# Row sums of a fused attention kernel: one more tile pair summed by DMA in each second half, and the output product moved in front of unit 59

## The reference

```python
Q, K, V = (proj(Wq), proj(Wk), proj(Wv))             # 16 heads of 32 channels
att = jnp.einsum('bhqd,bhkd->bhqk', Q, K) * (1.0 / math.sqrt(Dh)) + b[0]
att = att * m + (1.0 - m) * NEG_INF
att = jax.nn.softmax(att, axis=-1)
y = jnp.einsum('bhqk,bhkd->bhqd', att, V)            # then back to B x 512 x T
q = round(y / scale)                                 # int8 per row, scale = absmax / 127
out = x + float16((q @ weight.T) * scale * w_scale + bias)
```

## Time and profile before

| | |
|---|---|
| median of three runs | 2285.32 us |
| the profiled execution | 2288.77 us |
| its span, first to last instruction | 2287.0 us |
| granted TensorE clock | 0.996 of full |
| busy: TensorE / VectorE / ScalarE / GpSimd | 2264.2 / 1610.9 / 1298.3 / 1686.9 us |
| TensorE matmuls and weight loads | 12140 and 12172 |
| DMA moved | 432.24 MB, of it 166.73 MB in GpSimd's queue |

### The profile page before, as it was taken

The page is one execution under the profiler, slowest core; times in us unless marked ns, Lnnn a source line. Parts: engine busy times, 40 slices in busy tenths (PEclk is TensorE's granted clock), DMA queues, the critical chain, the costliest instruction groups (busy, mean ns, idle before and its releaser), DMA issues.

```text
span 2287.0 us, 34843 instructions
## 1 busy us (share of the span) xinstructions
PE 2264.2 (99%) x12140; PEld 1376.8 (60%) x12172; DVE 1610.9 (70%) x2779; ACT 1298.3 (57%) x2471; POOL 1686.9 (74%) x704
## 2 busy tenths in 40 slices
PE   9999999999999999999999999999999999999998
PEld 7888888887555555555555555555555555555553
DVE  3311111117788888888888888888888888888883
ACT  3322222223666666666666666666666666666664
POOL 2322333222689999899998998989998899899896
PEclk9999999999999999999999999999999999999999
DMA  6765455475788888888888888888888888888864
GB/s 238 254 230 194 177 190 212 183 229 141 157 183 181 194 192 192 191 191 187 188 182 188 191 193 190 188 185 194 191 192 189 187 193 186 179 193 196 189 149 102
DMA packets 146405, 432.24 MB, mean 189 GB/s; under 512 B 13192, under 2 KB 49032, under 8 KB 125904
## 3 DMA queue, kind: packets, MB, share of 16 engines
q1 hardware_dynamic: 114000, 237.31, 36.4%
q0 software_dynamic: 22896, 166.73, 36.3%
q10 hardware_dynamic: 9360, 26.22, 3.4%
HBM read 161.51 MB, written 100.93 MB: 115 GB/s over the span
## 4 chain that ended last, share of the span: by engine, by line
PE 96%; DMA 2%; issue 1%; POOL 1%; ACT 0%; DVE 0%; ACTq 0%; POOLq 0%
PE score L793 22%; PE ring L143 20%; PE pv L819 20%; PE ring L340 11%; PE score L340 9%; PE ring L865 5%; PE pv L340 3%; PE ring L832 2%; DMA probs<-probs 1%; PE ring L830 1%; POOL acc L1145 1%; PE ring L855 1%; PE ring L165 0%; ACT probs L927 0%; PE ring L842 0%
## 5 line engine op out<-in xcount | busy, mean ns | idle before, releaser
L150 DVE TENSOR_REDUCE half_max<-ring 128x1 f32<-128x512 f32 x2048 | 1256.7, 678 | 67.6 <-PE ring L143 59.9
L927 ACT ACTIVATE probs<-score 128x512 f32<-128x512 f32 x2039 | 1033.3, 615 | 471.7 <-PE score L793 466.2
L1145 POOL TENSOR_TENSOR acc<-acc,probs 128x2048 f32<-128x2048 f32 x189 | 898.9, 4756 | 62.5 <-DMA probs<-probs 61.8
L793 PE MATMUL score<-q_stack,k_stack 100*128 100x512 f32 x2039 | 847.6, 417 | 4.7 <-ACT probs L927 4.7
L143 PE MATMUL ring<-k_stack,q_stack 98*128 98x512 f32 x2048 | 816.6, 399 | 2.4 <-issue 2.2
L793 PEld LDWEIGHTS score<-q_stack,k_stack 100*128 100x128 f32 x2039 | 384.4, 189 | 331.8 <-issue 185.5
L819 PE MATMUL pv<-probs,v_in 128*32 128x512 f32 x4096 | 495.0, 601 | 0.0
L143 PEld LDWEIGHTS ring<-k_stack,q_stack 98*128 98x128 f32 x2048 | 389.4, 190 | 70.3 <-DVE qT L1052 8.7
L1145 POOL TENSOR_TENSOR acc<-probs 128x2048 f32<-128x2048 f32 x63 | 288.0, 4571 | 53.9 <-DMA probs<-probs 47.8
L558 POOL TENSOR_TENSOR q_stack<-x_raw,k_stack 128x1024 fp32r<-128x1024 f32 x28 | 67.9, 2471 | 293.9 <-ACT k_stack L422 293.9
L819 PEld LDWEIGHTS pv<-probs,v_in 128*32 128x32 f32 x4096 | 107.1, 109 | 233.1 <-ACT probs L927 145.2
(11 more groups left out here) (117 smaller groups left out, 1986.9 us busy)
## 6 DMA issues: line engine op xcount, KB each, us to landing
probs<-probs POOLq DMA_DIRECT2D x159, 1024.0 KB, 8.3
q_stack<-qk_part SPq DMA_DIRECT2D x192, 256.0 KB, 5.7
k_stack<-qk_part SPq DMA_DIRECT2D x96, 512.0 KB
qk_part<-part_hi SPq DMA_DIRECT2D x64, 512.0 KB, 2.7
qk_part<-part_lo SPq DMA_DIRECT2D x64, 512.0 KB, 3.6
v_steps<-v_out SPq DMA_DIRECT2D x64, 256.0 KB, 2.3
v_in<-v_steps SPq DMA_DIRECT2D x32, 512.0 KB, 5.6
v_out<-x ACTq DMA_DIRECT2D x31, 512.0 KB, 3.5
```

The lines of the kernel that those rows point to most:

```text
L150: nc.vector.tensor_reduce(half_max[:, pair // CHUNK, pair % CHUNK, half:half + 1], bank[:, :], AX_X, ALU.max, negate=True).then_inc(neg_ma ...
L793: pe.matmul(score[score_bank(s, t)][:, :], k_stack[par][0:ROWS, h, kt * P:(kt + 1) * P], q_stack[par][0:ROWS, half, h, :], start=True, sto ...
L927: nc.scalar.activation(probs[:, kt, h, :], score[score_bank(s, t)][:, :], ACT.Exp).then_inc(exp_done, 1)
L1145: nc.gpsimd.tensor_tensor(acc[:, half, :, :], first, probs[:, tile, :, :], ALU.add).then_inc(acc_done, 1)
```

## The change

The pair (2,3) is added to the list of transfers. First halves keep the pairs (0,1), (4,5), (6,7) and their additions. Second halves now transfer (0,1), (2,3), (4,5), and GpSimd adds tiles 6, 3, 5, 7 in that order. TensorE's product with tile 7 goes. GpSimd's order changes around the end of a step. The turned integers move from behind unit 55 to behind unit 54, and the output product from behind unit 59 (after weighing and sums) to behind the maximum of unit 58. The last step takes other banks for its last sums.

```diff
-PAIRS_OF_TILES = ((0, 1), (4, 5), (6, 7))
+PAIRS_OF_TILES = ((0, 1), (2, 3), (4, 5), (6, 7))
+PAIRED = ((0, 2, 3), (0, 1, 2))
-ADDED = ((2, 3, 5, 7), (2, 3, 5, 6))
-APART = 7
+ADDED = ((2, 3, 5, 7), (6, 3, 5, 7))
-TURN_1, SUMS_1, TURN_0, TURN_Q, SUMS_0 = 20, 27, 52, 55, 59
-FFN, SKEW = SUMS_0, SUMS_1
+TURN_1, SUMS_1, TURN_0, TURN_Q, FFN, SUMS_0 = 20, 27, 52, 54, 58, 59
+SKEW = SUMS_1
 EXTRAS = {TURN_1: ("turn",), SUMS_1: ("sums",), TURN_0: ("turn",), TURN_Q: ("turn_q",),
-          SUMS_0: ("unused", "sums", "ffn0", "ffn1")}
+          FFN: ("ffn0", "ffn1"), SUMS_0: ("unused", "sums")}
@@ sum_rows
-                if half == 1:
-                    for h in range(GH):
-                        pe.matmul(buf[h * DH:(h + 1) * DH, 0:N], ones[:, :], probs[:, APART, h, :], start=True, stop=False)
@@ TensorE, step
                     if t == GH - 1 and prev:
                         for kt in (QH * TT - 2, QH * TT - 1):
                             weigh(s - 1, 1 - par, kt)
+                    if t == FFN and prev:
+                        ffn(s - 1)
                     if t % BURST == GH - 1 and t > GH:
...
-                    if t == FFN and prev:
-                        ffn(s - 1)
@@ ScalarE, exps
-                    elif kt in READ_BY:
-                        wait(act, pair_done[READ_BY[kt]], 16 * pairs_before(s, half, READ_BY[kt]))
                     else:
-                        wait(act, sum_done, before + 1)
+                        wait(act, pair_done[kt // 2], 16 * pairs_before(s, half, kt // 2))
@@ GpSimd, step
+                if prev:
+                    add(s - 1, 1, 1)
                 if second:
                     add_bias(s - 2, 0)
                     add_residual(s - 2, 0)
...
                 add(s, 0, 3)
                 if ahead:
+                    begin_pair(s, 1, 1)
+                    begin_pair(s, 1, 2)
                     add(s, 1, 0)
-                    begin_pair(s, 1, 1)
-                    add(s, 1, 1)
```

More of the change, by code:

```diff
@@ L657, in pairs_before, with turned_q @@
         def pairs_before(s, half, i):
-            return s + half if PAIRS_OF_TILES[i][1] == APART else QH * s + half
+            return s * sum(i in paired for paired in PAIRED) + half * (i in PAIRED[0])
+        def turned_q(s):
+            return ("turn", TURN_0) if s >= LAST - 1 else ("turn_q", TURN_Q)
         def ring_of(use):
@@ L827, in sum_rows @@
                 pe.wait_ge(acc_done, ADDS * halves_before(s, half) + ADDS)
-                if half == 1:
-                    for h in range(GH):
-                        pe.matmul(buf[h * DH:(h + 1) * DH, 0:N], ones[:, :], probs[:, APART, h, :], start=True, stop=False)
                 for h in range(GH):
-                    mm = pe.matmul(buf[h * DH:(h + 1) * DH, 0:N], ones[:, :], acc[:, half, h, :], start=half == 0, stop=True)
+                    mm = pe.matmul(buf[h * DH:(h + 1) * DH, 0:N], ones[:, :], acc[:, half, h, :], start=True, stop=True)
                 mm.then_inc(sum_done, 1)
@@ L852, in turn_q @@
                     pe.wait_ge(last_q_done, 1)
-                buf16 = take_ring(s + 1, ("turn_q", TURN_Q))[:, :].bitcast(BF16)
+                buf16 = take_ring(s + 1, turned_q(s))[:, :].bitcast(BF16)
                 for tt in range(TT):
@@ L889, in step @@
                     if not ahead and t == UNITS - 13:
-                        last_sums = take_ring(s, ("sums", SUMS_0))
+                        last_sums = take_ring(STEPS, ("sums", SUMS_1))
                         sum_tile(2, last_sums, start=True)
@@ L894, in step @@
                             sum_tile(tile, last_sums)
-                    if t == FFN and prev:
-                        ffn(s - 1)
                     if not ahead and t == UNITS - 1:
-                        pe.wait_ge(prod_done, 2 * LAST - 1)
-                        sum_rows(s, 0, ring_of(("ffn0", FFN)))
+                        sum_rows(s, 0, take_ring(s, ("sums", SUMS_0)))
                         for kt in (QH * TT - 2, QH * TT - 1):
@@ L1051, in take_qT @@
                 wait(dve, ffn_done, 2 * s)
-                nc.vector.tensor_copy(qT[:, :, :].rearrange("p a b -> p (a b)"), ring_of(("turn_q", TURN_Q))[:, :].bitcast(BF16)[:, 0:T]).then_inc(qT_out, 1)
+                nc.vector.tensor_copy(qT[:, :, :].rearrange("p a b -> p (a b)"), ring_of(turned_q(s))[:, :].bitcast(BF16)[:, 0:T]).then_inc(qT_out, 1)
             def scale_product(s, half):
@@ L1086, in step @@
                         take_qT(s - 1)
-                    if t == SUMS_0 and ahead:
-                        recip(s, 0, ring_of(("sums", t)))
                     if t == FFN and prev:
@@ L1091, in step @@
                             scale_product(s - 1, half)
+                    if t == SUMS_0 and ahead:
+                        recip(s, 0, ring_of(("sums", t)))
             for s in range(STEPS):
                 step(s, s % 2, prev=s > 0, ahead=s < LAST)
-            recip(LAST, 0, ring_of(("ffn0", FFN)))
+            recip(LAST, 0, ring_of(("sums", SUMS_0)))
             spread(LAST, 0)
@@ L1098, in _ @@
             take_floor(LAST)
-            recip(LAST, 1, ring_of(("sums", SUMS_0)))
+            recip(LAST, 1, ring_of(("sums", SUMS_1)))
             spread(LAST, 1)
@@ L1133, in add @@
                 tile = ADDED[half][k]
-                if tile in SUMMED_BY:
-                    pool.wait_ge(pair_done[SUMMED_BY[tile]], 16 * (pairs_before(s, half, SUMMED_BY[tile]) + 1))
+                if tile % 2 == 1 and tile // 2 in PAIRED[half]:
+                    pool.wait_ge(pair_done[tile // 2], 16 * (pairs_before(s, half, tile // 2) + 1))
                 else:
@@ L1138, in add @@
                 if k == 0:
-                    pool.wait_ge(pair_done[SUMMED_BY[FIRST]], 16 * (halves_before(s, half) + 1))
+                    pool.wait_ge(pair_done[0], 16 * (halves_before(s, half) + 1))
                     wait(pool, sum_done, halves_before(s, half) - 1)
@@ L1179, in step @@
                 add(s, 0, 0)
-                begin_pair(s, 0, 1)
+                begin_pair(s, 0, 2)
                 add(s, 0, 1)
@@ L1185, in step @@
                     add_bias(s - 2, 1)
-                begin_pair(s, 0, 2)
+                begin_pair(s, 0, 3)
                 add(s, 0, 2)
```

2 lines of the change are left out of this document (removed).

## The result

| | before | after |
|---|---|---|
| median, 4 runs each on one chip | 2286.62 us | 2402.87 us |
| lowest and highest | 2284.84, 2288.55 | 2399.03, 2405.48 |
| ratio | 1 | 1.0507 [1.0486, 1.0528] |
| span of the profiled execution | 2287.0 us | 2397.2 us |
| granted TensorE clock | 0.996 | 0.984 |

The forecast was 2268 us, the range ended at 2310. The kernel became 116 us slower, 4.0 us in each step. The page of after: busy time by engine, the shares of the chain that ended last, the group of transfer issues with its idle time, and the transfers themselves. The chain was 96% TensorE before.

The account below looks back on a forecast made before the run. TensorE bound the kernel, GpSimd about 2 us a step behind; afterwards GpSimd's circle would bind at 52.7 us. 53.27 - 52.7 = 0.57 us, x 31 = 17.7; 2285.3 - 17.7 = 2268 us, range 2251 to 2310.

Parts of the forecast that it names:

- Tile 7's product: TensorE's eight instructions ahead of unit 28's score: removing them saves 0.85 us a step, 26.4 us over 31 steps.
- The seam: On TensorE, where the output product meets its neighbours near units 58 to 60: moving it saves about 0.2 us a step.
- TensorE's own step is thus 52.2: TensorE's step after the change: 53.27 less 0.85 for tile 7 and 0.2 for the moved product, 52.2 us.
- is issued 1 to 2 us behind (2,3): Second half's (4,5) transfer: queues behind (2,3), beside K loads, needed about 15 us after issue; both effects cost 0.1 us a step.
- A closed circle that never needs TensorE: GpSimd's order through three awaited landings plus 29.2 us of other time: 52.6 us, taken as 52.7, sets the step.
- TensorE is tied to it: the exponential of tile 5: At unit 52 this exponential needs a GpSimd addition that ended 4.9 us earlier; GpSimd sliding about 4 us uses that slack.
- The landings: GpSimd's awaited (0,1), (6,7) and new (2,3) transfers: 8.0, 7.6 and 7.8 us, sum 23.4; median of all near 7.6.
- The third rival: Slower, DMA engines full: longer landings in GpSimd's circle, step 54.1 to 54.3 us, about 2312 us; chance 0.24.
- The fourth rival: The product ahead of unit 59 waits over 0.3 us for qT or its bank; forecast holds within 6 us; no separate chance.
- GpSimd no longer waits for TensorE at the (0,1) transfer: Sign: GpSimd waits instead for DMA at the second half's second addition, 1 to 3 us.

Follow-up runs that it names:

- e11: The kernel before without TensorE's product with tile 7 in second halves, nothing in its place: 2265.24 us, 0.9901.
- e2: The kernel before with only the output product moved behind unit 58's maximum and the turned integers to 54: 2299.55 us, 1.0060.
- e10: The changed kernel with the 16 output products issued behind unit 59's weighing, ahead of the sums, VectorE's scaling with them: 2310.80 us, 1.0105.
- e7: e1 with the store of the second output half issued from SyncE instead of ScalarE: 2305.26 us, 1.0079.
- e5: The changed kernel with the store of the second output half issued from SyncE instead of ScalarE: 2350.80 us, 1.0286.
- e1: The kernel before with the third transfer and GpSimd's new order, output product and turned integers left as before: 2309.96 us, 1.0115.
- e12: e1 with GpSimd's step reordered: bias and residual ahead of additions, second normalise ahead of the first half's second addition: 2262.96 us, 0.9887.
- e4: The changed kernel with GpSimd's two normalise sooner, behind the second half's second addition and ahead of the first half's second: 2496.59 us, 1.0925.
- e14: e5 with only VectorE's first absmax moved from unit 19 to 26: 2399.51 us, 1.0484.

## Why the prediction was wrong, step by step

- **Tile 7's product: 26.4 us forecast, 22 measured (e11).** Right mechanism. At its place, units 27 to 28, e11 gains the 0.86 us that the start times had given (0.85); 0.1 us is lost again between units 51 and 56, so that 0.76 us a step is left.
- **The seam: 0.2 us gained was forecast, with 0 to 0.3 as the range; the sign was wrong.** It loses 0.3 us (e2, units 58 to 60), and the whole move costs 13 us alone. The start of a product was priced by what stands before it (narrow or wide), but in its new place it waits for its bank: the load starts 0.12 us behind the reduction of unit 55 in every step. The prediction had named this wait ("the product's bank waits for the reduction of unit 55, which follows the copy") and put it at zero.
- **"TensorE's own step is thus 52.2", with the product moved, and no cost for the units behind it. This is the step that failed.** The 3.4 us of the product were taken as moved from one side of unit 59 to the other. Yet the weighing of unit 59 was one of the things it moved past, and `pv_done` of that weighing releases the (4,5) transfer. I wrote that this transfer "is issued 1 to 2 us behind (2,3)"; it was issued 6.1 us behind (1345.04, 1351.17), with four additions queued behind it. e10, in which the product and the weighing change places again, puts 92 us on it. What is also left out of the 52.2 is the clock: the prediction reckoned with full clock throughout, and the stops brought spells at half clock worth some 22 us.
- **"A closed circle that never needs TensorE".** It is not shown, but it fits e7, where the store's wait is gone and the product is at its old place: GpSimd waits there for landings, and the sum comes within 0.9 us of the step. In the changed kernel the circles that bind go through TensorE. One runs from the weighing of unit 59 through GpSimd's queue up to the second `normalise` (about 37 us), VectorE's second `absmax` and TensorE's units 40 to 59 (about 19 us). The other leaves the same queue at the residual addition (46 us), and goes by ScalarE's store to TensorE's units 52 to 59 (about 11 us). e5 opens only the second and gets 52 us back.
- **"TensorE is tied to it: the exponential of tile 5".** I named one tie and there were more. I followed buffers (a tile is freed by an addition) and not queues: VectorE's `absmax` and ScalarE's store wait for GpSimd's small jobs, and reductions and exponentials that need neither stand behind them. In the profile before, these waits were there, small (9.1 us in 3 waits for `absmax`), and that was read as no tie. At the store there was no wait before, but the slack was only 1.8 us on average and 0.3 at the least.
- **The landings.** The median over all transfers was 8.1 us, not 7.6. But the three of the circle came out as forecast: their means are 7.3, 8.1 and 8.1 us, in sum 23.5 against 23.4. By the prediction's own sum the circle would have allowed 52.7 us, and the step was 57.2. The third rival, full DMA engines, had its price near 2312 and a chance of 0.24, and did not happen: the median landing was 8.1 and K rows were not awaited (unit 20 comes at 15.55 us of a step, before at 15.53). That slower came true was for another reason, at more than four times the price.
- **The fourth rival** (product waits for its bank in its new place) was right about the seam. It was put at "within 6 us", as it too priced only the wait at the product and nothing behind it.
- **What would show it.** "GpSimd no longer waits for TensorE at the (0,1) transfer" held there, but the wait for `pv` did not go to DMA; it went to the (4,5) transfer and tripled (54.9 to 163.1 us).

Not settled: how e1's 23 us divide between the store, the landings and the clock (e7, which removes the store's wait, gives back only 5), and how the 116 us divide between two circles that share one queue.

## What to carry to other kernels

When work is moved past an instruction that signals, price the signal, not only the work: find who waits for it, and what stands behind that waiter in its in-order queue. An engine with slack against the bound can still set the step if its small jobs are awaited at the head of another engine's queue; list those waits with their slack before reordering it, however small they are in the profile. The order of small jobs in such a queue is worth measuring (e12: 47 us against e1 by order alone). A job that stands between an issue and the instruction that needs its landing costs less than one ahead of the issue (e4: 48 us more of waits for landings). And where TensorE gets new stops, look at the granted clock of the steps, with and without a spell at half clock, before looking for a further cause (e14).

## What the runs showed of the hardware

- A bf16 product of 128 columns of weights starts 0.77 us behind narrow float32 matmuls where no wait for another engine shows (before), while score and maximum matmuls in float32 of 512 columns follow each other at 0.235 us. Its price behind a wide matmul is not known from these runs: the 0.59 us of e2 hold a wait for its bank.
- 16 DMA engines at 96% busy over 1500 us (210 GB/s) landed 1 MB accumulating transfers in 8.4 us at the median, against 8.3 at 84%. The median hides the tail: in e12 (4,5) of the second half, issued 1.6 us behind (2,3), took 14.0 us on average, 6.0 of them behind the landing of (2,3).
- The granted clock fell with the stops of TensorE: 1.00 in the steps of e12 (7 us idle in 1500), 0.98 in those of the changed kernel (70 in 1530), 0.97 in e14's (65 in 1530), and 0.966 over the whole of e4, the slowest. Before, in steps 5 to 27, TensorE's matmuls were never idle for more than 0.16 us and no spell at half clock occurred.
